# Loop bodies of eight edge tiles for VectorE and TensorE in the gathered sums

## The reference, cut to what matters

```python
x = layernorm(x + edge_gat(x, src, dst, edge_attr))       # attention: 4 heads, softmax over a node's edges, batch norm
x = layernorm(x + gcn(x, ...))                            # two convolutions, 512 -> 256 -> 512
x = layernorm(x + sage(x, ...))                           # weighted mean of neighbours, two products
x = layernorm(x + conv(x, ...))                           # sum over source nodes, one product
# the core of each: segment_sum(table[index_of_edge] * weight_of_edge, node_of_edge, num_segments=3125)
```

## Time and profile before

| | |
|---|---|
| median of 3 runs | 5218.31 us (5214.13 to 5221.86) |
| the profiled execution's own time | 5201.22 us |
| its span | 5199.4 us |
| attention sums (949 to 1600) | 651 us |
| g1, g2 (1857 to 2490, 2541 to 3170) | 633 and 629 us |
| g3, g4 (3479 to 4136, 4400 to 5081) | 657 and 681 us |

### The profile page before, as it was taken

The page is one execution under the profiler, slowest core; times in us unless marked ns, Lnnn a source line. Parts: engine busy times, 40 slices in busy tenths (PEclk is TensorE's granted clock), DMA queues, the critical chain, the costliest instruction groups (busy, mean ns, idle before and its releaser), DMA issues. The chain is left out here.

```text
span 5199.4 us, 61626 instructions
## 1 busy us (share of the span) xinstructions
PE 3186.2 (61%) x11552; PEld 1623.4 (31%) x11552; DVE 2743.3 (53%) x6786; ACT 840.1 (16%) x2383; POOL 2883.0 (55%) x2935
## 2 busy tenths in 40 slices
PE   6566663677885365555355554287767626777678
PEld 5334442344442233323133322142222212222224
DVE  8455554666665444444444443285555514555555
ACT  1111110566665320000000000120000013000004
POOL 8555556466664446666566666516556571555550
PEclk8677776799997676766666666698787767777779
DMA  3111111555652333323433332035555502555553
GB/s 125 50 56 40 56 42 35 180 165 166 170 168 44 89 105 86 88 85 87 107 87 86 87 86 55 21 90 169 164 161 169 149 10 76 165 161 161 161 163 110
DMA packets 219871, 555.53 MB, mean 107 GB/s; under 512 B 65386, under 2 KB 73202, under 8 KB 219440
## 3 DMA queue, kind: packets, MB, share of 16 engines
q0 software_dynamic: 165664, 438.90, 30.9%
q1 hardware_dynamic: 54112, 115.44, 6.8%
HBM read 507.95 MB, written 46.19 MB: 107 GB/s over the span
## 5 line engine op out<-in xcount | busy, mean ns | idle before, releaser
L1318 PE MATMUL g_part<-g_rows,g_hot 128*128 128x256 f32 (+1 forms) x3328 | 1633.8, 634 | 1054.7 <-DVE g_hot L1282 554.9
L1303 DVE TENSOR_TENSOR k_acc<-k_acc,g_part 128x256 f32 (+1 forms) x1664 | 921.1, 554 | 881.5 <-issue 511.5
L1318 PEld LDWEIGHTS g_part<-g_rows,g_hot 128*128 128x128 f32 x3328 | 717.8, 242 | 1970.7 <-issue 1027.8
L1275 POOL DMA_INDIRECT g_rows<-x,g_index x832 | 789.6, 949 | 788.9 <-ACT g_index L1262 249.2
L1282 DVE TENSOR_SCALAR g_hot<-k_columns,k_rec 128x128 f32<-128x128 f32 x1254 | 454.1, 362 | 324.5 <-issue 211.3
L1073 PE MATMUL at_part<-at_rows,at_hot 128*128 128x512 f32 x832 | 500.7, 694 | 144.7 <-DVE at_hot L1085 68.0
L1275 POOL DMA_INDIRECT g_rows<-x_scaled_w,g_index x416 | 394.8, 949 | 310.6 <-PE g_part L1318 118.0
L610 POOL DMA_INDIRECT edges_by_dst<-fr_records,f_dst_slots x392 | 378.5, 966 | 315.4 <-DVE fr_records L802 197.6
L1038 POOL DMA_INDIRECT at_rows<-h_table,at_index x416 | 397.0, 954 | 279.6 <-PE at_part L1074 112.4
L1275 POOL DMA_INDIRECT g_rows<-hidden_scaled,g_index x416 | 395.6, 951 | 239.9 <-PE g_part L1318 105.4
L180 POOL DMA_INDIRECT edges_by_src<-k_src_records,k_src_slots x392 | 390.4, 996 | 217.5 <-issue 117.6
(11 more groups left out here) (328 smaller groups left out, 3473.2 us busy)
## 6 DMA issues: line engine op xcount, KB each, us to landing
f_rows<-low_rows SPq DMA_DIRECT2D x28, 896.0 KB
x<-n_out SPq DMA_DIRECT2D x75, 256.0 KB
g_rows<-x,g_index POOLq DMA_INDIRECT x832
n_x<-x SPq DMA_DIRECT2D x50, 256.0 KB
at_rows<-h_table,at_index POOLq DMA_INDIRECT x416
g_rows<-x_scaled_w,g_index POOLq DMA_INDIRECT x416
g_rows<-hidden_scaled,g_index POOLq DMA_INDIRECT x416
f_x_in<-in_x SPq DMA_DIRECT2D x25, 256.0 KB
```

What stands on the lines that cost most here:

```text
L1275: pool.indirect_dma_start(rows[:, n, :], None, table, bass.IndirectOffsetOnAxis(index[:, h, n:n + 1], 0)).then_inc(gathered[n], 16)
L1303: dve.tensor_tensor(here, here, part[n % RING][:, 0:width].unsqueeze(1), ALU.add).then_inc(added, 1)
L1318: pe.matmul(part[u % RING][:, 0:width], hot[:, u % RING, :], rows[:, u % BT, :], start=True, stop=True).then_inc(summed, 1)
```

## The change

VectorE's and TensorE's loops of these stages have bodies of eight tiles. In `aggregate` they run 52 times, not 26, with one group of bucket numbers in a VectorE body. In `attention_sums` they run 51 times in the loop and write eight tiles out behind it. The loops of POOL and ScalarE stay at sixteen. What is waited for, and the order of the work within an engine, stay as they were; the buffer numbers fit, as eight is a multiple of four.

```diff
-        def edge_tiles(eng, step):
-            with eng.Fori(0, TILES // U - 1) as i:
-                for r in range(U):
-                    step(i * U, r, True)
-            for r in range(U):
-                step(TILES - U, r, False)
+        def edge_tiles(eng, step, each=U):
+            with eng.Fori(0, TILES // each - 1) as i:
+                for r in range(each):
+                    step(i * each, r, True)
+            for r in range(each):
+                step(TILES - each, r, False)
...
-                edge_tiles(pe, step)
+                edge_tiles(pe, step, BT)
...
-                    if more or r + AHEAD < U:
+                    if more or r + AHEAD < BT:
...
-                edge_tiles(dve, step)
+                edge_tiles(dve, step, BT)
...
-                with dve.Fori(0, TILES // BT // 2) as i:
-                    g = i * 2
-                    for h in range(2):
-                        tile = bucket_registers(nc, mybir.EngineType.DVE, buckets, g * BT + h * BT)
-                        for n in range(BT):
-                            u = h * BT + n
...
+                with dve.Fori(0, TILES // BT) as g:
+                    tile = bucket_registers(nc, mybir.EngineType.DVE, buckets, g * BT)
+                    for u in range(BT):
...
-                with pe.Fori(0, TILES // BT // 2) as i:
-                    g = i * 2
-                    for u in range(2 * BT):
+                with pe.Fori(0, TILES // BT) as g:
+                    for u in range(BT):
...
-                        pe.wait_ge(gathered[u % BT], g * 16 + (u // BT + 1) * 16)
+                        pe.wait_ge(gathered[u], g * 16 + 16)
```

More of the change, by code:

```diff
@@ L1289, in _ @@
                     weigh(n, n)
-                with dve.Fori(0, TILES // BT // 2) as i:
-                    g = i * 2
-                    for h in range(2):
-                        tile = bucket_registers(nc, mybir.EngineType.DVE, buckets, g * BT + h * BT)
-                        for n in range(BT):
-                            u = h * BT + n
[L1297 to L1304, removed]
+                with dve.Fori(0, TILES // BT) as g:
+                    tile = bucket_registers(nc, mybir.EngineType.DVE, buckets, g * BT)
+                    for u in range(BT):
+                        dve.wait_ge(summed, g * BT + (u + AHEAD - RING + 2 * BT + 1))
+                        weigh(g * BT + (u + AHEAD), u + AHEAD)
+                        dve.wait_ge(summed, g * BT + (u + 2 * BT + 1))
+                        dve.wait_ge(added, g * BT + (u + RING))
+                        here = acc[:, bass.ds(tile[u], 1), 0:width]
+                        dve.tensor_tensor(here, here, part[u % RING][:, 0:width].unsqueeze(1),
+                                          ALU.add).then_inc(added, 1)
             @block.tensor
```

## The result

The changed kernel is slower: 5297.95 us median of 4 runs (5291.78 to 5315.53), against 5220.09 (5214.13 to 5227.76) for the kernel before, measured beside it. The ratio is 1.0153, 95% interval 1.013 to 1.0177, so +78 us (68 to 92). The forecast was +34. The profiled execution took 5296.65 us, span 5294.9, against 5201.22 and 5199.4: +95.

A forecast was written before the change was run, and what follows sets the result against it. It took POOL's gathers, held up by slow stretches of VectorE's sequencer, to bound the sums. Added turns cost 27 us in aggregate and 7 in the attention, so 5218 + 34 = 5252 us, range 5218 to 5310.

The forecast's parts named there:

- What bounds the kernel: Sums: no engine busy throughout; POOL alone needs 520 us a stage, and VectorE's slow stretches lose 110 to 160 more.
- Cause of the slowness: VectorE's sequencer in the sums: POOL issuing without a pause makes it slow; the loop body's size is irrelevant.
- R1: Rival, chance 0.28: the long body makes VectorE slow; halving it gives 4690 us, or 4950 if half the stretches go.
- The turn: VectorE's aggregate loops: each added turn costs 1.05 us in the mean; 104 turns make 109 us if all exposed.
- How much is on the path: VectorE in aggregate: 0.13 to 0.35 of added time shows; with 0.25, 109 us becomes 27 us.
- The term for `aggregate`: VectorE's 104 added turns in g1 to g4: 27 us of the forecast's 34.
- TensorE, nothing: Aggregate: TensorE has its added branches done while waiting for `hot`, so 0; without that cover 31 us.
- Attention, 7 us: Attention sums: 26 more turns at 0.56 us are 15 us, half of it on the path.
- The signs: If right: 208 VectorE branches in aggregate, body's top about 1.75 us, as many slow stretches, g1 to g4 each 3 to 15 us longer.
- R2: Rival, chance 0.20: POOL's full buffers absorb every added turn; within 10 us of 5218.
- R4: Rival, chance 0.04: slow stretches catch the loop's top each time; +100 to +195 us, 5320 to 5410.
- R3: Rival, chance 0.10: another body breaks the stretches' rhythm and cuts one in ten short; -40 us, 5180.

The follow-up runs named there:

- r1: The kernel before, unchanged, run once more in a session without slow stretches; ratio 1.0001 (0.9992 to 1.0011) against itself.
- t2: Marks built over 256 columns, of which 128 are used, against the kernel before, with slow stretches: 5226.42 us, ratio 1.0006 (0.9987 to 1.0024).
- e1: Bodies of eight for VectorE alone, TensorE's left at sixteen, against the kernel before: ratio 1.0127 (1.0072 to 1.0183), +66 us.
- e2: Bodies of eight for TensorE alone, VectorE's left at sixteen, against the kernel before: ratio 0.9979 (0.9953 to 1.0006), -11 us.
- session 1: Follow-up session with slow stretches that ran e1, e2, e3 and e5 beside the kernel before, which took 5185.92 us (25 runs).
- e3: Bodies of 32 tiles for both VectorE and TensorE, against the kernel before: ratio 0.9934 (0.9910 to 0.9959), -34 us.
- e5: Old bodies of sixteen with six unused semaphore increments added to VectorE's aggregate body, against the kernel before: ratio 1.0070 (1.0044 to 1.0096), +36 us.
- t3: POOL at most six tiles ahead in g1 to g4, not eight, against the kernel before, with slow stretches: 5228.59 us, ratio 1.0011.

## Why the prediction was wrong in its size

- **What bounds the kernel.** Right for the condition in which it was measured: the slow stretches of the earlier trace rows hold POOL, and without them (r1) the sums fall to POOL's 520 us, as worked out there.
- **Cause of the slowness.** Half right. The body's length isn't it: bodies of 8, 16 and 32 all have the stretches (34, 30 and 31 in g1), so R1 falls. POOL's issuing, which the prediction took as the cause, goes with them (896 of 905 slow instructions), but is at most one condition of two: in r1 POOL issues without a pause and nothing is slow. Two readings of the prediction were loose, and nothing hangs on them: ScalarE's activations in the earlier trace rows start 0.70 and 1.40 us apart in turns before they settle at 1.40, and beside the 49 instruction packets of q8 the page has 46 on q14.
- **The turn.** 0.56 us quick and 3 us slow, 1.05 in the mean, with two turns in ten slow. The quick price is in the trace (1.74 us at the top). Of the 208 turns 22 to 29 were slow, 0.11 to 0.14, so by the prediction's own two prices the mean is 0.82 to 0.90 us. The 3 us were not measured by themselves.
- **How much is on the path: the step that failed.** It took 0.25 of VectorE's added time as exposed, from stages that differ in VectorE's *busy* time: 384 against 284 us, 397 against 279. That is time of the datapath. t2 adds 110 us of just that and pays nothing, so even the 0.25 was too much for it, and the differences between the stages were of another origin; g3 and g4 have rows twice as wide, for TensorE and the DMAs too, but what makes the difference isn't shown. The time of a turn is time of the sequencer, and most of that is exposed. The term for `aggregate`, forecast at 27 us, measured 66 to 78, the whole of e1's cost and of the change's, as the attention has no part in it that can be seen. Over 104 turns that is 0.63 to 0.75 us a turn, more than the quick price of 0.56. Against the prediction's own 109 us it is a share of 0.6 to 0.7, and against 104 x 0.82 to 0.90 = 85 to 94 us, 0.7 to 0.9.
- **TensorE, nothing:** right (e2). **Attention, 7 us:** nothing, by session 1 (647.2 us in e1 against 647.7 to 649.4 in e2, e3 and e5). The trace of the changed kernel has 9 us more, but t2 and t3, whose attention is that of the kernel before, have 659.2 and 660.7, so that much comes without the turns. **Code, nothing:** 47 packets on q8, not 49.
- **The signs.** Branches and the tile at the body's top came as foretold. The stretches are not as many as before, but 127 against 110 in the four sums; in e1, whose cost is nearly the same, 114. So their number doesn't carry the cost by itself. The stages g1 to g4 grew by 11 to 25 us, not 3 to 15.
- **R2** (nothing) is what happens without slow stretches, but not because full buffers absorb the turns: POOL is not held there at all, it sets the pace (525 us a sum against 520), and VectorE has time to spare. **R4** came near only in where stretches start, not in its price. **R3** fell.

The page "Advanced Engine Details and Errata" of the Trainium skill (control flow timing) was cited for 108 ns a branch, 14 us in all. The branches measure 56 and 208 ns in the median. In e1 a turn of VectorE costs 0.51 us, several times its branch, and in e5 instructions without any branch cost 36 us.

## What to carry to other kernels

Ask of an added instruction whether it takes the datapath or the sequencer, and take its exposure only from a comparison that differs in that same resource. Where a trace shows idle time on "issue" with long register instructions, look at the sequencer first. In this kernel loop turns and semaphore increments then cost 0.35 to 0.6 us for about six instructions, 110 us of wider data instructions cost nothing that can be told, and larger bodies (-34 us) or constants in place of register values (-129 us) paid. Measure such a kernel in more than one session before deciding, since the gain may exist in one condition alone.

## What was not expected of the hardware

- The same kernel takes 5186 to 5226 us in some sessions and 4087 to 4097 in others, on chips that differ; but sessions 2 (4096.87) and 5 (5226.32) were given the same chip number, so it doesn't go by the chip alone. With the slow condition, sequencer instructions of VectorE, ScalarE and SP take about 0.7 us in stretches; without it no register, branch or semaphore instruction of these three does (50 to 74 ns for VectorE's branch in r1). What brings the condition stays open.
- In the slow condition 110 us more of VectorE's datapath over four sums cost nothing that can be told (-7 to +13 us), and 624 semaphore increments, of a median of 21 ns, cost 36 us.
- Straight code on VectorE had no register arithmetic of 0.7 us in the sums, and instead 174 stops of over 2.5 us between instructions, whose commonest lengths are 0.7 us apart. Instruction packets by themselves aren't their cause: the same kernel without slow stretches has 111 of them on q14 against 112, and no such stop.
